# Audio tower on one core: the experts' turns with the first norm, its transpose and the stacked queries at other places, tile rows loaded one turn earlier, and the query bias as one bf16 product

## What is computed

```python
def _expert(x, Wqkv, bqkv, Wo, bo, g1, be1, W1, bf1, W2, bf2, g2, be2):
    qkv = x @ Wqkv.T + bqkv
    q, k, v = (to_heads(t) for t in jnp.split(qkv, 3, axis=-1))    # 8 heads of 16
    attn = softmax(einsum('bhqd,bhkd->bhqk', q * scale, k))
    ctx = einsum('bhqk,bhkd->bhqd', attn, v) ... @ Wo.T + bo
    x = _layernorm(x + ctx, g1, be1)
    h = gelu(gelu(x @ W1.T + bf1) @ W2.T + bf2)
    return _layernorm(x + h, g2, be2)
```

## Time and profile before

| | us |
|---|---|
| runs, median of 3 | 3249.82 |
| the profiled execution's own time | 3245.33 |
| its span in the profile | 3243.5 |
| PE busy in the span | 2765.3 |
| ACT / DVE / POOL busy | 1882.0 / 1840.4 / 546.3 |

### The profile page before, as it was taken

How to read it: one execution, slowest core, us unless ns; L and a number is a source line. 1 busy time by engine, 2 the same in 40 slices (tenths; PEclk the granted TensorE clock), 3 DMA queues, 4 the chain that set the end, 5 groups by cost and what they waited for, 6 DMA issues and landing times.

```text
span 3243.5 us, 66796 instructions
## 1 busy us (share of the span) xinstructions
PE 2765.3 (85%) x24695; PEld 1942.8 (60%) x24695; DVE 1840.4 (57%) x4886; ACT 1882.0 (58%) x4218; POOL 546.3 (17%) x728
## 2 busy tenths in 40 slices
PE   7788785899998999899988977688888888888898
PEld 5456454566766666666666653465565656556676
DVE  4664666567666677666676732344544444454454
ACT  2232233577776777677676768377348644754343
POOL 2000003234234433433222130000000000000000
PEclk9886887899999999999999988799899989999998
DMA  5000005766566776675565520100000000000000
GB/s 209 1 10 30 1 6 196 235 203 197 181 182 195 214 220 191 193 223 180 171 175 160 154 99 6 44 1 1 14 11 1 1 14 5 1 1 14 6 1 6
DMA packets 162466, 304.09 MB, mean 94 GB/s; under 512 B 19729, under 2 KB 121226, under 8 KB 154442
## 3 DMA queue, kind: packets, MB, share of 16 engines
q1 hardware_dynamic: 158818, 293.69, 29.4%
q0 software_dynamic: 3328, 6.14, 0.6%
HBM read 227.00 MB, written 72.75 MB: 92 GB/s over the span
## 4 chain that ended last, share of the span: by engine, by line
PE 50%; DVE 15%; issue 11%; ACT 10%; DMA 4%; DVEq 4%; POOL 3%; POOLq 1%; PEld 1%; ACTq 1%; PEldq 0%; SPq 0%
PE ps L1870 4%; PE ps L1535 4%; PE ps L1553 4%; PE ps L1514 4%; DMA xg<-slots_x 4%; PE ps L1348 3%; PE ps L1940 2%; PE ps L2002 2%; PE ps L1578 2%; PE ps L1802 2%; PE ps L1587 2%; PE ps L1964 2%; ACT hid L2332 2%; PE ps L1333 2%; DVE peaks L2697 1%
## 5 line engine op out<-in xcount | busy, mean ns | idle before, releaser
L2697 DVE TENSOR_REDUCE peaks<-ps 128x1 f32<-128x748 f32 x608 | 557.1, 932 | 270.1 <-PE ps L1514 252.4
L2185 ACT ACTIVATE pt<-ps 128x384 f32<-128x384 f32 x1216 | 562.2, 491 | 193.7 <-PE ps L1535 178.1
L1535 PE MATMUL ps<-qst,kst 98*128 98x128 bf16 x3648 | 392.5, 224 | 14.9 <-ACT pt L2185 9.7
L1535 PEld LDWEIGHTS ps<-qst,kst 98*128 98x128 bf16 x3648 | 244.9, 99 | 171.0 <-ACT pt L2185 56.6
L1166 POOL TENSOR_TENSOR rstd<-var,minus_half 128x6 f32<-128x6 f32 x40 | 52.9, 1323 | 1668.1 <-DVE var L2602 1218.7
L1514 PE MATMUL ps<-kst,qst 96*128 96x374 bf16 x1216 | 305.6, 333 | 12.7 <-DMA kst<-saved_k 5.5
L1553 PE MATMUL ps<-pt,vst 128*32 128x128 f32 (+1 forms) x7296 | 273.1, 282 | 0.0
L1553 PEld LDWEIGHTS ps<-pt,vst 128*32 128x32 f32 (+1 forms) x7296 | 188.8, 112 | 89.6 <-issue 59.5
L1514 PEld LDWEIGHTS ps<-kst,qst 96*128 96x128 bf16 x1216 | 100.1, 100 | 26.1 <-DVE qst L2775 6.7
L2775 DVE CAST qst<-ps 96x1024 bf16<-96x1024 f32 x76 | 92.6, 1219 | 37.0 <-PE ps L1465 36.3
L1964 PE MATMUL ps<-xnT,QT 128*128 128x374 f32 (+5 forms) x256 | 94.4, 473 | 6.4 <-ACT shared L2382 5.1
(11 more groups left out here) (659 smaller groups left out, 6528.8 us busy)
## 6 DMA issues: line engine op xcount, KB each, us to landing
kst<-saved_k SPq DMA_DIRECT2D x76, 1176.0 KB
wf<-in_l SPq DMA_DIRECT2D x76, 512.0 KB
vst<-saved_v SPq DMA_DIRECT2D x76, 408.0 KB, 3.3
saved_k<-kparts SPq DMA_DIRECT2D x144, 192.0 KB, 3.9
saved_v<-vprod SPq DMA_DIRECT2D x32, 408.0 KB, 3.6
rows<-in_l_rows SPq DMA_DIRECT2D x76, 128.0 KB
saved_k<-kst SPq DMA_DIRECT2D x48, 192.0 KB, 2.7
slots_x<-zeros SPq DMA_DIRECT2D x4, 1216.0 KB, 11.4
```

The lines of the kernel that those rows point to most:

```text
L1535: mm = pe.matmul(out[:, c * P:(c + 1) * P], kst[0:STACK + SHIFT, m % 3, head, j * P:(j + 1) * P], qst[0:STACK + SHIFT, m % 3, head, :], st ...
L2185: act.activation(pt[:, u % (2 * GROUP), :], entry()[:, 0:H0], ACT.Exp, scale=float(HD) ** -0.5)\
L2697: v.tensor_reduce(peaks[:, g, head:head + 1], entry()[:, :, 0:T // 2], XY, ALU.max)\
```

## The change

It moves four steps in the list, and computes the query bias in another way.

- `load_x` loads tile n+4 instead of n+3 (still at place 4).
- `stack` goes from place 7 to place 11.
- `norm1` goes from place 14 to place 1 of the next turn, and `turn_x1` from place 1 to place 5.
- The query bias becomes one bf16 matmul. `bq` is loaded three times, to partitions 0, 32 and 64 of a cleared buffer (two more loads). In the opening, after expert 4's keys, DVE splits them into three bf16 parts and builds a one-hot with the row repeated every 32 partitions (`query_bias`). ACT's and PE's waits for the tables count 96 instead of 64, and the tables' loads wait for POOL's clears.

```diff
@@ opening_steps, turn_steps
+        if e == 4:
+            yield "bias_parts",
-    if 3 <= n + 3 < RUN:
-        put(4, ("load_x", n + 3))
+    if 3 <= n + 4 < RUN:
+        put(4, ("load_x", n + 4))
-        put(7, ("stack", early))
+        put(11, ("stack", early))
-        put(14, ("norm1", done))
     if 0 <= n - 2 < RUN:
-        put(1, ("turn_x1", n - 2))
+        put(1, ("norm1", n - 2))
+        put(5, ("turn_x1", n - 2))
@@ SP, load_tables
+                        sp.wait_ge(S["ramps_ready"], 2)
...
-                        sp.dma_start(bq[0:E, :], A["l1"][:, :, W1_BIAS], allow_slow_non_contiguous=True).then_inc(loaded, 16)
+                        for c in range(3):
+                            sp.dma_start(bq[PLACE * c:PLACE * c + E, :], A["l1"][:, :, W1_BIAS], allow_slow_non_contiguous=True)\
+                                .then_inc(loaded, 16)
@@ POOL, experts
+                pool.memset(bq[:, :], 0.0)
                 pool.drain().then_inc(S["ramps_ready"], 1)
@@ PE, query
+                    if m == 0:
+                        pe.wait_ge(S["bias_split"], 1)
                     out = bank()[:, 0:P]
                     pe.matmul(out, xgT[:, m % 2, :], wq[:, m % 2, :], start=True, stop=False)
-                    pe.matmul(out, onehot[0:E, m:m + 1].to_broadcast([E, P]), bq[0:E, :], start=False, stop=True)\
+                    pe.matmul(out, onehot_b[0:3 * PLACE, m:m + 1].to_broadcast([3 * PLACE, P]), bq_parts[0:3 * PLACE, :],
+                              start=False, stop=True)\
                         .then_inc(S["ring_ready"], 1)
@@ ACT, keys (PE's biases alike)
-                        act.wait_ge(S["tables_loaded"], 64)
+                        act.wait_ge(S["tables_loaded"], 96)
@@ DVE, experts
+                def query_bias():
+                    v.tensor_copy(lane_row[:, :], place[:, :])
+                    v.drain()
+                    for c in range(1, GROUP):
+                        v.tensor_scalar(beyond[:, :], place[:, :], float(PLACE * c), float(PLACE), ALU.is_ge, ALU.mult)
+                        v.drain()
+                        v.tensor_tensor(lane_row[:, :], lane_row[:, :], beyond[:, :], ALU.subtract)
+                        v.drain()
+                    v.tensor_scalar(onehot_b[:, :], whose_sum[:, :], lane_row[:, 0:1], None, ALU.is_equal)
+                    v.wait_ge(S["tables_loaded"], 96)
+                    v.tensor_copy(bq_rest[:, :], bq[:, :])
+                    v.drain()
+                    v.tensor_copy(bq_parts[:, :], bq_rest[:, :])
+                    v.drain()
+                    for c in range(1, 3):
+                        for i in range(c, 3):
+                            rows = slice(PLACE * i, PLACE * (i + 1))
+                            v.tensor_tensor(bq_rest[rows, :], bq_rest[rows, :], bq_parts[rows, :], ALU.subtract)
+                        v.drain()
+                        for i in range(c, 3):
+                            rows = slice(PLACE * i, PLACE * (i + 1))
+                            v.tensor_copy(bq_parts[rows, :], bq_rest[rows, :])
+                        v.drain()
+                    v.drain().then_inc(S["bias_split"], 1)
```

More of the change, by code:

```diff
@@ L104 @@
     "base_ready", "att_ready", "y_normed", "y_affine",
-    "query_part_ready",
+     "query_part_ready", "bias_split",
     "logits_ready", "exps_ready", "third_free", "fourth_loaded",
@@ L715, in audio_tower @@
         bq = sb("bq", [P, P])
+        bq_rest = sb("bq_rest", [P, P])
+        bq_parts = sb("bq_parts", [P, P], BF16)
+        lane_row = sb("lane_row", [P, 1])
+        beyond = sb("beyond", [P, 1])
+        onehot_b = sb("onehot_b", [P, RUN], BF16)
         kb = sb("kb", [P, E, BIAS_COLS])
@@ L1473, in biases @@
                         pe.wait_ge(S["routed"], 2)
-                        pe.wait_ge(S["tables_loaded"], 64)
+                        pe.wait_ge(S["tables_loaded"], 96)
                     out = bank()
@@ L2771, in experts @@
                         n.take("rounded_ready")
+                    elif what == "bias_parts":
+                        query_bias()
                     elif what == "peak":
```

## The result

The changed kernel takes 3261.72 us, median of 20 runs (3252.86 to 3271.87), beside 3246.22 us for the kernel before, also 20 runs (3234.05 to 3256.37). The ratio is 1.0047, with a 95% interval of 1.0035 to 1.0058. It is slower by some 15.5 us: under 1%, but well outside what the runs leave open. The forecast said 18 us faster.

The account below looks back on a forecast made before the run. PE's own stream was taken as the bound in the experts' stage. Terms -40 (x1n) - 24 (bias) - 9 (stack's wait) - 5 (xg) + 49 (cast) + 8 (stack's own time) + 3 (opening) = -18 us: 3230 us, range 3185 to 3268.

Parts of the forecast that it names:

- x1n: PE's wait at place 1 for DVE's norm1 goes: -40 us, low end 27 us.
- stack: wait for POOL, cast, own time: Stack moved to place 11: -9 us of POOL waits, +49 for DVE's cast, +8 for PE's own time.
- rows: Tile rows xg loaded a turn earlier: -5 us, between 0 and 17.9, as the peak behind may wait for keys.
- turns with gathers: Three turns where DVE's first merge waits for gathered rows whatever PE does: zero booked, low end -18 us.
- Query bias: One bf16 matmul for PE's f32 product saves 0.32 us in 76 turns: -24 us, ends 15 and 27.
- The stack's cast: PE waits 1.06 us at place 12's peak for DVE to empty the stack's banks: +49 us, between 0 and 60.
- The stack's own time: The stack's 0.45 us on PE in its new place, burst and other turns together: +8 us, between -5 and +15.
- Opening: Before ACT's first keys, two more bq loads and 14 small DVE instructions: +3 us, between 1 and 10.
- The cast costs more than the waits it removes: Rival: DVE late at the turn's end, divide waits for peaks in most turns; +39 us, 3285 us, chance 0.15.

Follow-up runs that it names:

- experiment 2: Kernel before with only norm1 moved to place 1 and x1n's transpose to place 5; 3238.65 us, ratio 0.9990.
- experiment 3: Kernel before with only the stack moved from place 7 to place 11; 3276.5 us, ratio 1.0107.
- Experiment 11: Changed kernel with the stack back at place 7 and the merges of gathered rows, with their store, one turn later; 3225.1 us, ratio 0.9951.
- experiment 8: Changed kernel with the stack back at place 7 and x1n's transpose at place 2 instead of 5; 3230.11 us, ratio 0.9962.
- 12: Changed kernel with the stack at place 9, x1n's transpose at place 2 and the merges one turn later; 3214.82 us, ratio 0.9924.

## Why the prediction was wrong

The direction was wrong: -18 us forecast, +15.5 measured. The views were the right ones and the mechanism of the loss was named; the sum failed in two of its terms, x1n's and the bias's, which both counted a gain whole.

| term | forecast | measured alone, by the medians | the stage in its profile |
|---|---|---|---|
| x1n | -40 | -5 | -2.1 |
| bias with its opening | -24 + 3 = -21 | -6 | -10.6, without the opening |
| stack: wait for POOL, cast, own time | -9 + 49 + 8 = +48 | +33 | +39.9 |
| rows | -5 | -6 | -3.6 |
| turns with gathers | 0 | within the others | +3.5, within the others |

- **Norm1 and its transpose: the step that failed.** "The wait goes. Its size is 38.2 to 50.7 us": it went, to 2.4 us. But the text priced only the wait at the old place and never the transpose at the new one. The order rows showed it between divide and the scores of place 6; what it meets there are 0.38 us of its own and 0.22 for ACT's copy of the shift, in bursts, key turns and plain turns alike. The profile of before held what was needed. Its 38.9 us are 42 waits in 76 turns; 10 of the 17 bursts have none. The price stands in all 76: -38.9 of waits, -16 of own cost at place 1 (76 x 0.21, the burst's figure), +46 at place 5 (76 x 0.60) is -9. On top of that the waits for DVE's peaks rose by 18.8 us in experiment 2, most of it in the three turns with merges, and POOL's by 2.1, while xg's fell by 6.6: +5 in sum, where the stage has -2.1 and the medians -5. So the account closes to some 10 us. It is enough to say that the gain is near zero, and that the low end should have stood there and not at 27 us.
- **Query bias: the size per turn was right, its worth was not.** I had 0.32 us a turn; it is 0.36 at the product, 0.31 over a plain turn. The failed sentence is "nothing has to be uncovered for it to count". It has: in 14 turns PE stands before the stack for POOL, in others for x1n, `xg` or a gather, and there a shorter row of PE only lengthens the wait. POOL's rose by 10.4 us and x1n's by 3.2.
- **The stack's cast: right.** 1.06 us in 46 to 57 turns, 49 in sum; measured 1.03 a turn (0.87 listed at the row, 46.0 us in 54 waits). "PE goes on at 1.96" was 1.92. That the waits for DMA would absorb it in 11 turns came true in another way: there are 53 or 54 waits and not 46, but in experiment 3 xg's wait fell by 10.2 us, where 11 x 1.06 is 12.
- **The stack's own time: right.** I booked +8; the stretches of experiment 3 give some 7.
- **The stack as a whole: 8 to 15 us too high.** Experiment 3's +33 is 15 under my +48, its stage's +39.9 only 8. POOL's wait gave 3.6 of it (12.6, where I had 9, since I had set 7 of the 16.3 aside with the gathers). The rest is within what the runs leave open, and no row shows it. By the medians it hid nearly half of the 35 us by which x1n was wrong, which is luck.
- **Rows: right.** 5 us, of a possible 0 to 17.9, measured 6 with an interval that reaches zero. The wait passed to `kst` for the most part: 17.9 became 11.4 us. By the rule of the Trainium skill ("DMA: Bandwidth & Descriptors", Queues, rings and completion order) that the text cited, a DMA's semaphore write lands only after the same DMA engine's earlier writes. The trace agrees in that two thirds of the wait passed on, though no run shows the keys' landing itself. How long before the rows the keys land, which the forecast took to be next to nothing, does not follow from the rule: the third of the wait that went, 6.5 us in 11 or 12 waits, is what the runs show of it.
- **Gathers.** I had the mechanism (DVE held at the first merge) and called it zero; the wait for peaks behind it is there, 20.2 us in 8 waits, up to 7.0, and DVE's own wait at the first merge grew from 5.1 to 18.2 us in three. The six turns are 3.5 us longer in sum, so the zero was nearly right. Experiment 11 shows that DVE is one keeper of these turns and POOL the next.
- **Opening: right, +3 us.** ACT's first keys start at 525.06 instead of 524.30, and the first `turn_x` is 1.1 us later. But SP's list of loads began 2.3 us earlier in this execution than in that of before; its start lies between 508 and 513 us in the 14 profiles, whatever the kernel. Before, and then now:

```profile
513.31 0.58 SPq L1090 DMA_DIRECT2D kb<-in_l  x1
...
510.98 0.58 SPq L1098 DMA_DIRECT2D kb<-in_l  x1
...
516.64 4.25 SPq L1102 DMA_DIRECT2D bq<-in_l  x3
```

  From the first table's load to ACT's first keys are 11.0 us before and 14.1 now; over all profiles 11.0 to 12.6 in the four without the new bias and 13.9 to 16.0 in the ten with it. That is 3 us for the two extra loads, bounded at 1.4 to 9.3. DVE's 16 instructions take from 546.13 to 550.42, 4.3 us where I had 4, and from ACT's first keys to the first `turn_x` next to nothing is added (0.2 us in the mean).

Of the rivals on the time none was what happened. "The cast costs more than the waits it removes" ended on the right side, but for another reason: divide waits for peaks in 11 turns only (11.2 us), not in most. Its low value for x1n, 27, was still five times the truth.

What stays open: experiment 8's and 12's local gains were seen to come back as waits for POOL, keys and norm, but which of these chains would have to be shortened first was not tried. Nor was the share of ring and ACT's own lateness in the 0.22 us tried apart, beyond place 2 being free of it.

## What to carry to other kernels

A step that is moved to end a wait has two prices, and the one at the new place must be read like a new instruction: its own distance in the stream there, and, where it takes a buffer of a ring, whose release the next user now gets instead. Where the bound engine stands for others in many of its turns, work taken from that engine is worth only what the turns without such a wait give. And a producer's place in a list has two sides: far enough from what feeds it (POOL, two places here) and far enough from the next user of its buffer (more than 1.9 us here: 2.43 at place 9 was enough; and more where other work stands ahead in the copying engine's queue). Place 7 failed the first, place 11 the second; with all else equal, places 8 and 9 were 11 to 12 us faster than the one and some 40 us faster than the other (39 by the ratios, 44 by the medians).

## What the runs showed of the hardware

DVE's instructions on one column take 0.15 to 0.16 us and follow each other at 0.23 us with a drain between them, as here in the opening of the changed kernel (I had taken 0.3 for each of its instructions, and the larger ones make up for it):

```profile
546.13 0.15 DVE L2777 COPY lane_row<-place 128x1 f32<-128x1 f32 x1
546.36 0.15 DVE L2780 TENSOR_SCALAR beyond<-place 128x1 f32<-128x1 f32 x1
```

A bf16 product of 96 rows costs PE 0.06 us in a stream, whereas its row says 0.22: the row's modelled duration overlaps the next. DVE's cast of 96x1024 from PSUM to bf16 takes 1.22 us, and PE goes on 1.92 us after the start of the first matmul that filled those banks.
